# Hybrid attention loop: key rotation on VectorE spread over three steps, router work gathered in step 7, and turned keys stored in two column orders

## The reference

```
q = rms_norm(x @ wq) ; k = rms_norm(x @ wk) ; v = x @ wv        16 query heads, 4 key heads, head 128
k_ctx = rms_norm(ctx @ wk_ctx) ; v_ctx = ctx @ wv_ctx           64 context positions, not rotated
q, k = q * cos + rotate_half(q) * sin, k * cos + rotate_half(k) * sin
scores = q . [k_ctx, k] / sqrt(128), causal on k only ; probs = softmax ; x = x + (probs @ v) @ wo
probs = softmax(layernorm(x) @ router_w.T) ; top1 weight and index of 32 experts ; then the expert's product
```

## Time and profile before

| | |
|---|---|
| median of 3 runs | 1252.36 us (1252.36 to 1252.71) |
| the profiled execution | 1250.75 us |
| its span, first to last instruction | 1248.9 us |
| hybrid loop in it, about | 500 to 1150 us from the span's start |
| one batch of the hybrid loop, batches 4 and 5 | 84.3 us |
| busy over the span | PE 85%, DVE 72%, ACT 52%, POOL 26% |
| mean granted TensorE clock | 0.941 of full |

### The profile page before, as it was taken

One profiled execution on the slowest core, in us unless ns is written; L12 is line 12 of the kernel. 1 busy time (PEld: TensorE's weight loads), 2 busy tenths in 40 slices (PEclk: granted clock), 3 DMA queues, 4 the chain that ended last, 5 costly groups with the idle time before them and its releaser, 6 DMA issues.

```text
span 1248.9 us, 22083 instructions
## 1 busy us (share of the span) xinstructions
PE 1060.5 (85%) x6399; PEld 729.9 (58%) x6407; DVE 894.2 (72%) x2522; ACT 645.0 (52%) x2011; POOL 324.4 (26%) x496
## 2 busy tenths in 40 slices
PE   3676788689989967989999999899999998998396
PEld 1444345566666644556666666666656666665285
DVE  4576677487788765886867967778678678665375
ACT  0434777455555633655556545555565555552262
POOL 0212321211232121322313213223133132111456
PEclk9955999999999988989999999999999999999598
DMA  9501000112122000400000000000000000000731
GB/s 306 202 0 34 1 1 1 51 53 52 51 58 84 27 1 4 146 1 13 1 6 9 1 14 1 1 14 1 6 9 1 13 1 1 13 1 16 256 91 47
DMA packets 38795, 49.58 MB, mean 40 GB/s; under 512 B 5030, under 2 KB 29484, under 8 KB 38448
## 3 DMA queue, kind: packets, MB, share of 16 engines
q1 hardware_dynamic: 36400, 44.31, 11.9%
...
...
## 4 chain that ended last, share of the span: by engine, by line
PE 37%; DVE 11%; issue 6%; POOL 3%; ACT 3%; DMA 0%; DVEq 0%; ACTq 0%; POOLq 0%
PE PS L1663 33%; POOL out_dram L1289 3%; DVE arena L746 2%; DVE arena L758 1%; DVE arena L722 1%; PE PS L2011 1%; PE PS L1988 1%; ACT arena L1505 1%; POOL tokens_dram L1265 1%; ACT arena L1514 1%; DVE arena L732 1%; DVE arena L728 1%; DVE small L780 0%; DVE early L655 0%; DVE early L650 0%
## 5 line engine op out<-in xcount | busy, mean ns | idle before, releaser
L1663 PE MATMUL PS<-EW,arena 128*128 128x128 f32 (+4 forms) x640 | 134.4, 341 | 18.0 <-DVE small L746 11.2
L1663 PE MATMUL PS<-early,arena 128*32 128x256 f32 (+6 forms) x856 | 105.1, 357 | 42.1 <-DVE early L612 23.7
L1663 PE MATMUL PS<-wq,EW 128*128 128x512 f32 x256 | 126.6, 617 | 12.6 <-DVE arena L722 12.3
L1203 POOL TENSOR_SCALAR small<-small 128x4 f32<-128x4 f32 x64 | 18.3, 286 | 427.4 <-ACT mask L1498 250.4
L1663 PEld LDWEIGHTS PS<-EW,arena 128*128 128x128 f32 x640 | 99.6, 193 | 48.9 <-issue 23.5
L746 DVE CUSTOM_DVE_ANT_0 arena<-PS,kmask 128x128 f32<-128x128 f32 (+3 forms) x256 | 92.4, 389 | 42.3 <-PE PS L1663 34.1
L1514 ACT ACTIVATE arena<-arena,small 128x128 f32<-128x128 f32 (+3 forms) x256 | 119.5, 471 | 1.3 <-DVE small L751 1.1
L1505 ACT ACTIVATE arena<-PS 128x512 f32<-128x512 f32 x64 | 38.2, 597 | 153.2 <-PE PS L1988 153.2
L1663 PE MATMUL PS<-wo,early 128*128 128x256 f32 x512 | 113.3, 380 | 2.5 <-DVE sinT L799 1.7
L1663 PEld LDWEIGHTS PS<-wo,early 128*128 128x128 f32 x512 | 97.2, 190 | 16.3 <-DVE sinT L799 2.1
L1663 PEld LDWEIGHTS PS<-early,arena 128*32 128x32 f32 (+3 forms) x864 | 49.8, 115 | 93.3 <-issue 45.5
...
## 6 DMA issues: line engine op xcount, KB each, us to landing
...
```

What stands on the lines that cost most here:

```text
L1663: return pe.matmul(dst, lhs, rhs, start=first, stop=last)
```

## The change

- **DVE.** `turn_key` 1 moves from step 4 to step 5, `turn_key` 2 from step 5 to step 6. `token_stats` moves from step 4 to step 7, `choose` from step 6 to step 7, both ahead of `hybrid_finish`; `keep_weight` goes behind it. `copy_logits` moves to the head of step 5, `keep_scales` to step 1 of the next batch. In batch 7 `token_stats` and `keep_scales` stay, `choose` moves to step 7 there too.
- **PE.** `turn_keys` 1 moves from step 5 to the head of step 6; `turn_keys` 2 moves from step 6 to step 1 of the next batch, into bank 7.
- **ACT.** `turned_keys` writes each block into two stores: eK0 for the first query half (one buffer) and eK1 for the second (one for each parity). Block 0 takes two copies, block 1 three, block 2 two, where each took one. `token_norm` moves from step 5 of the loop turn of batch b (for batch b-1) to step 0 of the next turn; `weights` goes ahead of `outputs` in step 7. POOL's `token_scales` moves to step 7.
- **Scores.** The new stores repeat 64 keys ahead of the context, so that tile 3 takes one product from column 0 and the others start at column 64. The widths become `SEEN`: 96, 128, 160, 192 for the first half and 224, 256, 288, 320 for the second. `masked_max` still reads `WIDTHS` columns; the columns that no product writes any more are under its mask.

```diff
--- before.py
+++ after.py
...
 WIDTHS = ((128, 128, 192, 192), (256, 256, 320, 320))
+SEEN = ((96, 128, 160, 192), (224, 256, 288, 320))
 STARTS = ((0, 128, 256, 448), (0, 256, 512, 832))
 NE = 32
 TOK = B * J
@@ -289,7 +290,8 @@
-        eKT = cut(3072, (2, XG, KEYS), F32, spare)
+        eK0 = cut(3072, (XG, 2 * P), F32, spare)
+        eK1 = [cut(4096, (XG, 3 * P), F32, spare), cut(1024, (XG, 3 * P), F32, spare)]
@@ -882,6 +884,8 @@
                     further = [i + k < 8 or nxt[0] == HYBRID for k in range(4)]
+                    if i == 5 and routed:
+                        copy_logits(b - 2, 7)
                     if i >= 2 or former:
                         turned_probs(u - 2, (i - 2) % 8)
                     if further[1]:
@@ -898,22 +902,28 @@
                     if i == 4:
                         if nxt[0] == HYBRID:
                             turn_key(nxt[1], 0)
-                            turn_key(nxt[1], 1)
                         if former:
                             hybrid_finish(b - 1, 1)
+                            if nxt[0] != HYBRID:
+                                token_stats(b - 1)
+                    if 5 <= i <= 6 and nxt[0] == HYBRID:
+                        turn_key(nxt[1], i - 4)
+                    if i == 1 and routed:
+                        keep_scales(b - 2)
+                    if i == 6 and nxt[0] != HYBRID:
+                        keep_scales(b - 1)
+                    if i == 7:
+                        if former and nxt[0] == HYBRID:
                             token_stats(b - 1)
-                    if i == 5 and nxt[0] == HYBRID:
-                        turn_key(nxt[1], 2)
-                    if i == 5 and routed:
-                        copy_logits(b - 2, 7)
-                    if i == 6 and former:
-                        keep_scales(b - 1)
-                    if i == 6 and routed:
-                        choose(b - 2)
-                    if i == 7:
                         if routed:
+                            choose(b - 2)
+                        if nxt[0] == HYBRID:
+                            hybrid_finish(b, 0)
+                            if routed:
+                                keep_weight(b - 2)
+                        else:
                             keep_weight(b - 2)
-                        hybrid_finish(b, 0) if nxt[0] == HYBRID else hybrid_last(b)
+                            hybrid_last(b)
                     if further[1]:
                         masked_max(u + 1, (i + 1) % 8, (2, 3))
                     if further[3]:
@@ -1238,7 +1248,7 @@
-                    if i == 5 and former:
+                    if i == (7 if more else 5) and former:
@@ -1448,10 +1458,16 @@
             def turned_keys(b, par, k, at=2):
                 n = P if k else T
-                start = T + (k - 1) * P if k else 0
                 act.wait_ge(e_kt, 3 * b + k + 1)
-                act.activation(eKT[:, par, :, start:start + n],
-                               PS[:, at, 0:XG * n].rearrange("p (g n) -> p g n", g=XG), ACT.Copy).then_inc(e_kc, 1)
+                src = PS[:, at, 0:XG * n].rearrange("p (g n) -> p g n", g=XG)
+                first = HALF + T + (k - 1) * P if k else HALF
+                if k < 2:
+                    act.activation(eK0[:, :, first:first + n], src, ACT.Copy)
+                if k == 1:
+                    act.activation(eK0[:, :, 0:HALF], src[:, :, HALF:P], ACT.Copy)
+                if k == 2:
+                    act.activation(eK1[par][:, :, 0:HALF], src[:, :, HALF:P], ACT.Copy)
+                act.activation(eK1[par][:, :, first:first + n], src, ACT.Copy).then_inc(e_kc, 1)
@@ -1584,27 +1600,29 @@
                     if i == 5 and more:
                         turned_keys(nxt[1], 1 - par, 0)
                     if i == 6 and more:
-                        turned_keys(nxt[1], 1 - par, 2)
+                        turned_keys(nxt[1], 1 - par, 1)
                     exps(u, i)
                     if further[3]:
                         query_squares(u + 3, (i + 3) % 8)
+                    if i == 7 and routed:
+                        weights(b - 2)
...
                         values(b, par, 1)
-                    if i == 7 and routed:
-                        weights(b - 2)
                     if i == 1 and more:
                         raw_keys(nxt[1], 1 - par, 0)
                     if i == 2 and more:
                         raw_keys(nxt[1], 1 - par, 1)
-                    if i == 5 and more:
-                        turned_keys(nxt[1], 1 - par, 1)
+                    if i == 1 and former:
+                        turned_keys(b, par, 2, 7)
                     if further[2]:
                         turned_query(u + 2)
-                    if i == 5 and former:
+                    if i == 0 and routed:
+                        token_norm(b - 2)
+                    if i == 5 and not more:
                         token_norm(b - 1)
@@ -1993,13 +2011,10 @@
                 pe.wait_ge(e_qc, v + 1)
                 for t in tiles:
                     after(pe, e_mx, GH * v + t - 1)
-                    full = WIDTHS[j][0]
-                    if t == GH - 1:
-                        product(PS[:, 4, 0:HALF], eQT[:, t * P:(t + 1) * P], eKT[:, par, g, full:full + HALF])
-                        product(PS[:, 4, HALF:HALF + full], eQT[:, t * P:(t + 1) * P], eKT[:, par, g, 0:full]).then_inc(e_s, 1)
-                    else:
-                        product(PS[:, 3 + t % 2, 0:WIDTHS[j][t]], eQT[:, t * P:(t + 1) * P],
-                                eKT[:, par, g, 0:WIDTHS[j][t]]).then_inc(e_s, 1)
+                    first = 0 if t == GH - 1 else HALF
+                    keys_of = eK1[par] if j else eK0
+                    product(PS[:, 3 + t % 2, 0:SEEN[j][t]], eQT[:, t * P:(t + 1) * P],
+                            keys_of[:, g, first:first + SEEN[j][t]]).then_inc(e_s, 1)
@@ -2090,7 +2105,7 @@
                     if i == 5 and more:
                         turn_keys(nxt[1], 0)
                     if i == 6 and more:
-                        turn_keys(nxt[1], 2)
+                        turn_keys(nxt[1], 1)
                     if further[3]:
                         raw_query(u + 3, (i + 3) % 8, pars[3])
                     if i == 2:
...
                         pe.wait_ge(e_vr, 2 * b + 1)
                         values(b, par, 1)
+                    if i == 1 and former:
+                        turn_keys(b, 2, 7)
                     if i == 1 and more:
                         keys(nxt[1], 1 - par, 0)
                     if i == 2 and more:
                         keys(nxt[1], 1 - par, 1)
+                    if i == 2 and former:
+                        pe.wait_ge(e_kc, 3 * b + 3)
                     if i == 2 and routed:
                         token_turn(b - 2, 7)
                     if i == 6 and not more:
@@ -2114,9 +2133,6 @@
                         pe.wait_ge(f_lg, b)
                     if i == 4 and former:
                         hybrid_out(b - 1, 1)
-                    if i == 5 and more:
-                        pe.wait_ge(e_kc, 3 * b + 4)
-                        turn_keys(nxt[1], 1)
                     if i == 7:
                         hybrid_out(b, 0)
                     if i == 7 and not more:
@@ -2135,9 +2151,9 @@
                         if i == 4 and former:
                             pe.wait_ge(s_x, HYBRID * B + b)
                         if i == 5 and more:
+                            pe.wait_ge(e_kc, 3 * b + 4)
+                        if i == 6 and more:
                             pe.wait_ge(e_kc, 3 * b + 5)
-                        if i == 6 and more:
-                            pe.wait_ge(e_kc, 3 * b + 6)
                         if i == 7:
                             pe.wait_ge(e_yf, b + 1)
                         turn_query(u + 2, (i + 2) % 8)
```

2 lines of the change are left out of this document (1 added, 1 removed).

## The result

The changed kernel took **1261.63 us**, median of four runs (1257.89 to 1262.20), beside 1252.53 us of the kernel before on the same chip: ratio 1.0063, 95% interval 1.0041 to 1.0085. Twelve later runs gave 1256.90 us (1253.09 to 1263.35) and 1.0051 (1.0033 to 1.0068). By these ratios the change costs 6 to 8 us; I had forecast 1250.4 us and "within 0.2%" or faster with 0.75. The profiled execution took 1257.89 us, its span is 1256.1 us against 1248.9 before; it was the shortest of the four, so the trace explains 7.2 us and not the whole distance of the medians.

The account below looks back on a forecast made before the run. PE was taken to bound the kernel nearly everywhere, DVE's chain only between the projections of steps 4 and 7. Terms 1.6 + 1.9 - 2.4 - 1.7 - 0.7 - 0.7 = -2.0 us gave 1250.4 us, range 1243 to 1259.

Parts of the forecast that it names:

- The tight stretch: From `hybrid_finish` of step 4 to `raw_query` of step 7, where DVE's chain sets the time: +0.3 us per batch.
- the wait for the exponentials: In step 5 DVE reaches `normalise` before ACT's exponentials end and waits 0.6 us.
- the waits ahead of tile 0: Sign: PE waits 1.4 to 2 us ahead of tile 0's scores in step 6 and again in step 7.
- The wide stretch: The other 62 us of a batch, set by PE's own work: -0.35 us per batch, seven times -2.4.
- the wait of `raw_query` in step 1: PE's 0.32 us wait for the rotation behind DVE's maxima of tile 3, forecast to go.
- ACT becomes the wait: Rival: steps 1, 5 and 6 wait for ACT, 1.2 us per batch, 1258.8 us; chance 0.15.
- The ends: Terms outside the steady batches: batch 0 -1.7, batch 1 +1.9, batch 7 -0.7, the start -0.7 us.
- The start: -0.7: The start and batch 0's first steps: -0.7 us from smaller products, some at half clock.
- Batch 0 without the half clock: Sign: step 4 of batch 0 loses one rotated block (2.73 us) and PE keeps its full clock.
- my case: The main forecast, the sum of all terms: 1250.4 us, "within"; chance 0.40.
- My rival: The clock falls in step 6 behind PE waits of 1.4 to 1.9 us: 7 x 1.5, 1261 us; chance 0.08.
- spread, but out of its cover: One more `turn_key` block, 2.74 us, stands behind `hybrid_finish`; before, it stood in step 4 where DVE waited anyway.

Follow-up runs that it names:

- c_keys45: The changed kernel with DVE's `turn_key` put back to steps 4, 4 and 5: 1243.03 us, ratio 0.9919 to the kernel before.
- b_router: The kernel before with the router's moves alone, rotation and scores as before: 1243.83 us, ratio 0.9927 to the kernel before.
- e_fill7: The changed kernel with unread identity products filling PE's waits in step 7 only, four and four: 1253.42 us, ratio 1.0023 to the kernel before.
- e_fill6: The changed kernel with five unread identity products ahead of tile 0 in step 6 only: 1263.52 us, ratio 1.0101 to the kernel before.
- g_key7: The changed kernel with key blocks 0 and 1 rotated in step 4 and block 2 in step 7: 1224.44 us, ratio 0.9792 to the kernel before.
- e_fill: The changed kernel with unread identity products filling PE's waits in steps 6 and 7: 1258.11 us, ratio 1.0039 to the kernel before.

## Why the prediction was wrong

**The order of VectorE's work: right.** The tight stretch was to grow by 0.3 us and grew by 0.20 to 0.33 in batches 3 to 6. Its terms too: the wait for the exponentials 0.46 us for 0.6; the waits ahead of tile 0 1.75 and 1.12 for "1.4 to 2". Shown by c_keys45: a rotation behind `hybrid_finish` costs the batch 2.20 us. I had reckoned the moves of the router against it, and b_router shows those alone at -1.86 us per steady batch. Two edits of nearly equal size and other sign is what the change is.

**The wide stretch: right in its sign, too large in its size.** -0.35 us per batch was forecast; from `raw_query` of step 7 to that of the next step 4, batch 5 has 51.22 us for 51.50. Without the falls, batches 1 to 6 have -0.13 to -0.28 and batch 0 has +0.26, together -1.0 us for -2.4. Two points were off: the wait of `raw_query` in step 1 stays (0.26 for 0.32) and the one for ACT's copy in step 1 grows (0.50 for 0.33). The rival "ACT becomes the wait" did not come: its price was 1.2 us per batch in the tight stretch, and that grew by 0.33 at most, with 0.46 us of waiting for ACT in it. Its margin was as thin as I said: in step 6 of batch 4 the exponentials end 0.1 us before DVE comes for them.

**The ends: right up to the clock.** Batch 0, steps 4 to 7: forecast -1.7, measured 26.72 us for 28.41, -1.69. Batch 1: forecast +1.9 in steps 4 to 7, measured 32.71 for 30.95, +1.76. Batch 2 was taken as steady (+0.3) and had +0.95 there, since the kernel before was 0.5 us shorter there than in later batches (8.22 for 8.73 us from step 6 to 7), which I hadn't looked up. Batch 7 up to the last projection: forecast -0.7, measured -0.80, although its wait grew to 2.78 us. "The start: -0.7" can't be judged: the `raw_query` of step 4 in batch 0 starts at 524.4 and 526.7 us in the two profiles of the changed kernel, and at 524.4 to 529.5 over all traces. "Batch 0 without the half clock" was wrong: it moved from step 5 to step 7.

**The step that failed is the granted clock.** I put the chance of falls at 0.08, placed them in step 6 only, and charged nothing for them in my case, with the reason that 1.49 and 1.75 us had brought none. The rows show falls in step 7 behind 1.30 and 0.99 us (batch 0) and behind 1.12 and 1.07 us (batch 6), with score products of 0.8 to 0.9 us between them. Measured: 4.8 us of the 7.2 us of span in the profiled execution, 3.1 of them in step 7 and 1.7 in the last projection. e_fill7, which fills step 7 alone, gives 3.1 us of span and 3 to 5 us by the ratios; the last projection's part no run tested by itself. My rival gave 1261 us, which is near the measured 1261.63 by luck and not by its mechanism: its falls in step 6 happened (two in the profile) and cost nothing, because DVE is later there; the ones that cost stand in step 7 and in the tail, which I hadn't looked at. The Trainium skill (TensorE: Matmul & The Clock Gate, "Why this matters for your kernels") warns of long idle gaps; here shorter ones, two in a row, went with the fall, and a wait of 1.49 us with one of 1.07 before the change didn't. The measurement decides: in this kernel waits far shorter than the 3.59 us of the earlier trace rows can be followed by a fall.

Without the falls the profiled execution would be some 2.4 us above the one of before, of which 1.2 is ahead of the loop. Without those of step 7 alone it would be 4.1 us above, which is what e_fill7's trace has (1253.0 for 1248.9 us). The 2.4 us lie 4.4 us above my sum of -2.0: 1.9 is the start (+1.2 for -0.7), 1.4 the wide stretch (-1.0 for -2.4), 0.9 lies behind the last projection, where I had nothing, and 0.4 the tight stretches of batches 2 to 6 (+2.0 for +1.6, which should have read 1.5). Not settled is which waits bring a fall in which execution: the changed kernel's two profiles have it at different batches, batches 3 to 5 have the same 1.12 and 1.07 us without one, 3.50 us of waits had no fall in the kernel before and five in e_fill6, and the last projection falls behind 2.78 us here but not in g_key7 and e_fill.

The second thing that I passed over: I called the rotation "spread, but out of its cover" and priced it, but didn't ask where the cover was. The trace had it: 5.40 us of DVE ahead of `hybrid_finish` in step 7, where 3.92 us were left after the router's work had moved there.
